# One TensorE product per Householder reflection, an eigenvalue search by leading minors in two rounds, and new intervals between the small products

## The reference

```
x = x + L0(h)   # normalized adjacency, W1, batch norm, relu, W2, batch norm
x = x + L1(h)   # two graph convolutions, then four LSTMs over windows of 1, 2, 3, 4 nodes
x = x + L2(h)   # U (relu((U^T h) W1 + b1) W2 + b2), U the eigenvectors of the 64x64 normalized Laplacian
x = x + L3(h)   # three convolutions with adj*adj: W1 (256), W2 (512), W3 (128)
```

## Time and profile before

| what | value |
|---|---|
| median of 3 runs | 1024.05 us (1023.99 to 1024.16) |
| profiled execution | 1024.09 us, span 1022.3 us, mean granted clock 0.950 |
| PE busy | 861.4 us (84%) |
| DVE busy | 591.2 us (58%) |
| ACT busy | 527.1 us (52%) |
| POOL busy | 333.1 us (33%) |

### The profile page before, as it was taken

One profiled execution on the slowest core, in us unless ns is written; L12 is line 12 of the kernel. 1 busy time (PEld: TensorE's weight loads), 2 busy tenths in 40 slices (PEclk: granted clock), 3 DMA queues, 4 the chain that ended last, 5 costly groups with the idle time before them and its releaser, 6 DMA issues.

```text
span 1022.3 us, 12192 instructions
## 1 busy us (share of the span) xinstructions
PE 861.4 (84%) x3721; PEld 569.7 (56%) x3721; DVE 591.2 (58%) x2897; ACT 527.1 (52%) x962; POOL 333.1 (33%) x404
## 2 busy tenths in 40 slices
PE   2678578298979999799877989966899999999998
...
DMA packets 2961, 13.26 MB, mean 13 GB/s; under 512 B 464, under 2 KB 464, under 8 KB 2640
## 3 DMA queue, kind: packets, MB, share of 16 engines
...
## 4 chain that ended last, share of the span: by engine, by line
PE 55%; DVE 27%; POOL 8%; ACT 7%; issue 3%; DMA 0%; SPq 0%; DVEq 0%; ACTq 0%; POOLq 0%
PE PS L390 54%; POOL BIG L853 7%; ACT T L756 2%; DVE ST L1361 2%; ACT BIG L795 1%; DVE stats L1333 1%; DVE Fq L1170 1%; DVE Fq L1167 1%; DVE PS L1119 1%; ACT BIG L787 1%; DVE sc L1050 1%; ACT BIG L772 1%; DVE vcol L1047 1%; DVE T L1457 1%; DVE PS L1123 1%
## 5 line engine op out<-in xcount | busy, mean ns | idle before, releaser
L390 PE MATMUL PS<-BIG,wts 128*128 128x512 f32 (+2 forms) x1264 | 438.1, 500 | 37.6 <-POOL BIG L853 21.8
L390 PEld LDWEIGHTS PS<-BIG,wts 128*128 128x128 f32 x1264 | 239.9, 195 | 198.1 <-issue 112.7
L853 POOL TENSOR_TENSOR BIG<-BIG 128x256 f32<-128x256 f32 (+2 forms) x272 | 254.8, 943 | 247.8 <-ACT BIG L787 183.0
L787 ACT ACTIVATE BIG<-PS,lbias 128x256 f32<-128x256 f32 (+2 forms) x312 | 165.2, 558 | 102.6 <-PE PS L390 102.0
L694 ACT ACTIVATE BIG<-PS 128x1024 f32<-128x1024 f32 x64 | 65.5, 1023 | 88.9 <-PE PS L390 88.9
L694 ACT ACTIVATE T<-PS 128x512 f32<-128x512 f32 x96 | 55.1, 593 | 98.6 <-PE PS L390 98.6
L702 ACT ACTIVATE T<-X,shift,rstd 128x128 f32<-128x128 f32 x192 | 78.3, 482 | 52.4 <-DVE shift L1349 52.4
L1472 DVE TENSOR_TENSOR X<-X,PS 128x512 f32<-128x512 f32 x64 | 43.4, 682 | 107.1 <-PE PS L390 87.1
L390 PE MATMUL PS<-T,wts 128*128 128x512 f32 x192 | 100.3, 653 | 1.0 <-ACT T L694 0.7
L1493 DVE TENSOR_TENSOR T<-PS,wts 128x512 f32<-128x512 f32 x16 | 11.1, 691 | 150.9 <-PE PS L390 150.9
L841 POOL TENSOR_SCALAR rstd<-mv 128x4 f32<-128x4 f32 x48 | 10.9, 228 | 234.6 <-DVE mv L1340 234.6
...
## 6 DMA issues: line engine op xcount, KB each, us to landing
X<-x_in SPq DMA_DIRECT2D x1, 4096.0 KB, 12.8
...
```

The source lines that it names most:

```text
L390: return nc.tensor.matmul(o, l, r, start=start, stop=stop)
L787: nc.scalar.activation(LB[:, q, {"i": I_, "g": G_, "f": F_, "o": O_}[g], 0:n], PS[:, 3 * q + rank[q] % 3, 0:n], ACT.Tanh if g == "g" else ...
L853: nc.gpsimd.tensor_tensor(out, a, b, op).then_inc(pool_set[q], 1)
```

## The change

One product per reflection: `row_product` and NI are gone. The next pivot row is computed on VectorE, from the old row of S (which TensorE brings together with the av product, `old_row`) and the two rank-one terms of the present reflection; the norm and the other sums are made from it on VectorE, and the updates of S run beside the next reflection (`update`, `aside`). The search has two rounds: the first spreads 4096 shifts over all partitions and counts for all eigenvalues at once, the second looks at 64 shifts for each. Leading minors (products, rescaled once half way) take the place of quotients, without a reciprocal in each step. The factorizations from both ends run as one chain, the lower 64 partitions forwards and the upper 64 backwards, in four segments with rescaling; one more product (`ways`) brings both to all partitions. The planner's intervals and its prices of the LSTM products are new. The order of layer 1's own work, layers 2 and 3 and all DMAs but the size of the constants are as before.

```diff
-ROUNDS = 3
+ROUNDS = 2
...
-PACE = 2.5
-PACE_ROW = 1.8
-PACE_AV = 4.9
-PACE_GRID = 38.0
-PACE_TWIST = 45.0
+PACE = 3.0
+PACE_AV = 8.0
+PACE_GRID = [40.0, 32.0]
+PACE_TWIST = 27.0
+PACE_SCAN = 13.0
+SMALL = 0.5
+SHORT_ROUND = 1.6
...
-            def row_product(k):
-                pe.wait_ge(hh_x, k + 1)
-                mm(eb(0)[:, 0:NODES + 1 - k], S[0:NODES, k:k + 1].broadcast_to((NODES, P)),
-                   NI[0:NODES, k + 1:NODES + 2]).then_inc(hh_row, 1)
+            def old_row(o, k):
+                n = NODES - 1 - k
+                return mm(o[:, 0:n], ident[0:NODES, k:k + 1].broadcast_to((NODES, P)), S[0:NODES, k + 1:NODES])
             def av_product(k):
                 pe.wait_ge(hh_v, k + 1)
+                if k + 1 < REFLECTIONS:
+                    old_row(eb(3), k + 1)
                 mm(eb(2)[:, 0:NODES - k], vcol[0:NODES, 0:1].broadcast_to((NODES, P)), S[0:NODES, k + 1:NODES + 1])\
                     .then_inc(hh_av, 1)
...
-                    yield PACE_ROW
-                    row_product(k)
                     yield PACE_AV
                     av_product(k)
...
-                    yield PACE_GRID
+                    yield PACE_GRID[n]
                     pe.wait_ge(grid_cnt, n + 1)
-                    mm(eb(2)[:, 0:1], C("fold"), sc[:, 3:4]).then_inc(grid_sum, 1)
+                    if n == 0:
+                        mm(eb(2)[:, 0:1], tmp[:, :], ones[:, 0:1]).then_inc(grid_sum, 1)
+                    else:
+                        mm(eb(2)[:, 0:1], C("fold"), sc[:, 3:4]).then_inc(grid_sum, 1)
...
                 yield PACE_TWIST
+                pe.wait_ge(prep_dve, PREP["ways"])
+                prep(mm(eb(0)[:, 0:P], C("fold"), both_ways[:, :]))
+                yield PACE_SCAN
...
+            old_row(eb(0), 0).then_inc(hh_row, 1)
...
-                row_product(r)
...
+                clock[0] += SMALL
                 due[0] = None if pace is None else max(due[0], clock[0] - 1.0) + pace
...
-                            spend(n * 4 * (1 + (s > 0)) / 2400)
+                            spend(n * 4 * (2 if s else 1.25) / 2400)
+                        if s == 0 and p > 2:
+                            spend(SHORT_ROUND)
...
+            def update(k, in_psum):
+                trail = S[:, k + 1:NODES]
+                z = (eb(1) if in_psum else zrow)[:, 0:NODES - 1 - k]
+                first = op(v.scalar_tensor_tensor(trail, z, vn, trail, ALU.mult, ALU.add))
+                yield
+                dve.wait_ge(hh_ops, first)
+                op(v.scalar_tensor_tensor(trail, row_of(k, in_psum), zn, trail, ALU.mult, ALU.add))
+                yield
...
-                head, trail = S[:, k:k + 1], S[:, k + 1:NODES]
-                v0, vr, av = eb(0)[:, 0:1], eb(0)[:, 0:m], eb(2)[:, 0:m]
-                xm = NI[:, NODES:NODES + 1]
-                dve.wait_ge(hh_S, k + 1)
-                v.tensor_scalar(NI[:, NODES:NODES + 2], C("below")[:, k:k + 2], head, None, ALU.mult)\
-                    .then_inc(hh_x, 1)
...
-                small_product()
-                dve.wait_ge(hh_row, k + 1)
-                copied = v.tensor_copy(sc[:, 36:38], eb(0)[:, m:m + 2])
...
+                xr, trail = row_of(k, False), S[:, k + 1:NODES]
+                x0 = xr[:, 0:1]
+                vr = xr if by_pool else row_of(k, True)
...
+                def aside():
+                    behind = update(k - 1, k > REFLECTED) if k else iter(())
+                    next(behind, None)
+                    rest = op(v.tensor_tensor_reduce(junks[:, 0, 0:m - 1], xr[:, 1:m], vr[:, 1:m], 1.0, 0.0, ALU.mult,
+                                                     ALU.add, r2))
+                    yield
+                    op(v.tensor_scalar(sg, x0, 0.0, 2.0, ALU.is_gt, ALU.mult))
+                    yield
+                    next(behind, None)
+                    yield
+                    op(v.tensor_tensor_reduce(junks[:, 1, 0:m], vr, ident[:, k + 1:NODES], 1.0, 0.0, ALU.mult, ALU.add, xc))
+                    yield
+                    dve.wait_ge(hh_ops, rest)
+                    op(v.tensor_scalar(guard, r2, TINY, 1e30, ALU.is_lt, ALU.mult))
+                    yield
+                off = aside()
+                squares = v.tensor_tensor_reduce(junks[:, 2, 0:m], xr, vr, 1.0, 0.0, ALU.mult, ALU.add, n2)
                 if by_pool:
-                    copied.then_inc(hh_norm2, 1)
+                    squares.then_inc(hh_norm2, 1)
+                    for _ in off:
+                        next(beside, None)
+                    next(beside, None)
+                    next(beside, None)
+                    dve.wait_ge(hh_norm, k + 1)
+                    need(hh[0], beside)
                 else:
-                    op(copied)
...
+                    got = op(squares)
+                    next(off)
+                    need(got)
+                    got = op(v.tensor_scalar(y_.bitcast(I32), n2.bitcast(I32), -0.5, float(0x5F3759DF), ALU.mult, ALU.add))
+                    next(off)
+                    need(got)
...
-                op(v.tensor_scalar(vcol[:, :], C("next")[:, k:k + 1], beta, xm, ALU.mult, ALU.subtract))
-                op(v.tensor_scalar(v0, v0, beta, None, ALU.add))
-                sync()
...
-                v.tensor_tensor_reduce(junk[:, 0:m], trail, vr, 1.0, 0.0, ALU.mult, ALU.add, S[:, NODES:NODES + 1])\
...
+                v.tensor_tensor_reduce(junks[:, 3, 0:m], trail, vr, 1.0, 0.0, ALU.mult, ALU.add, S[:, NODES:NODES + 1])\
...
-                sync()
...
-                op(v.tensor_scalar(vcn, vcol[:, :], nc_, -1.0, ALU.mult, ALU.mult))
-                dve.wait_ge(hh_v, k + 1)
...
-                op(v.tensor_scalar(wp, S[:, NODES:NODES + 1], nc_, -1.0, ALU.mult, ALU.mult))
-                sync(1)
-                op(v.tensor_scalar(vcnn, vcn, nc_, -1.0, ALU.mult, ALU.mult))
...
+                need(op(v.tensor_scalar(hd, x0, beta, guard, ALU.mult, ALU.max)), beside)
+                need(op(v.reciprocal(nc_, hd)), beside)
+                op(v.tensor_scalar(half_nc, nc_, -0.5, None, ALU.mult))
+                op(v.tensor_scalar(a0, x0, nc_, -1.0, ALU.mult, ALU.mult))
+                op(v.tensor_scalar(vn, vcol[:, :], nc_, -1.0, ALU.mult, ALU.mult))
...
-                op(v.tensor_scalar(wcol[:, :], vcnn, eb(2)[:, m:m + 1], wp, ALU.mult, ALU.add))
-                op(v.scalar_tensor_tensor(trail, av, vcn, trail, ALU.mult, ALU.add))
-                sync()
-                v.scalar_tensor_tensor(trail, vr, wcol[:, :], trail, ALU.mult, ALU.add).then_inc(hh_S, 1)
+                dve.wait_ge(hh_v, k + 1)
+                need(hh[0])
+                need(op(v.tensor_scalar(kappa, eb(2)[:, m:m + 1], half_nc, None, ALU.mult)), beside)
+                got = op(v.scalar_tensor_tensor(zrow[:, 0:m], xr, kappa, eb(2)[:, 0:m], ALU.mult, ALU.add))
+                op(v.tensor_scalar(zc, vcol[:, :], kappa, S[:, NODES:NODES + 1], ALU.mult, ALU.add))
+                need(got, beside)
+                psum = k + 1 > REFLECTED
+                if k + 1 < REFLECTIONS:
+                    op(v.tensor_scalar(b0, zrow[:, 0:1], nc_, -1.0, ALU.mult, ALU.mult))
+                    got = op(v.scalar_tensor_tensor(eb(1)[:, NODES:NODES + m - 1], zrow[:, 1:m], a0, eb(3)[:, 0:m - 1],
+                                                    ALU.mult, ALU.add))
+                    if psum:
+                        op(v.scalar_tensor_tensor(eb(1)[:, 0:m], xr, kappa, eb(2)[:, 0:m], ALU.mult, ALU.add))
+                    need(got, beside)
+                    for p_ in range(2 if k + 1 >= REFLECTED else 1):
+                        got = op(v.scalar_tensor_tensor(row_of(k + 1, p_), xr[:, 1:m], b0, eb(1)[:, NODES:NODES + m - 1],
+                                                        ALU.mult, ALU.add))
+                    op(v.tensor_scalar(zn, zc, nc_, -1.0, ALU.mult, ALU.mult))
+                    need(got, beside)
+                else:
...
+                    gop(v.memset(Z[:, HALF, :], 1.0))
+                    gop(v.tensor_scalar(xn, C("grid" if r else "spread"), s1(2), s1(1), ALU.mult, ALU.add))
                     gsync()
-                    gop(v.tensor_tensor(Qh[:, :, :], eb(0)[:, 0:NODES].unsqueeze(2).broadcast_to([P, NODES, M]),
-                                        xg[:, :].unsqueeze(1).broadcast_to([P, NODES, M]), ALU.subtract))
+                    gop(v.tensor_scalar(Z[:, HALF - 1, :], xn, d[:, 0:1], None, ALU.add))
+                    gop(v.tensor_scalar(Z[:, HALF + 1, :], xn, d[:, NODES - 1:NODES], None, ALU.add))
+                    for i in range(1, HALF):
+                        j = NODES - 1 - i
+                        up, dn = HALF - i, HALF + i
+                        gsync(1)
+                        gop(v.scalar_tensor_tensor(ta, xn, d[:, i:i + 1], Z[:, up, :], ALU.add, ALU.mult))
+                        gsync(1)
+                        gop(v.scalar_tensor_tensor(tb, xn, d[:, j:j + 1], Z[:, dn, :], ALU.add, ALU.mult))
```

(89 more changed lines are left out.)

200 lines of the change are left out of this document (102 added, 98 removed).

## The result

| | before | changed |
|---|---|---|
| median, us | 1024.06 (1023.99 to 1024.16, 4 runs) | 1056.45 (1055.23 to 1064.93, 4 runs) |
| ratio | | 1.0334, 95% interval 1.0280 to 1.0388 |
| profiled execution, us (its span) | 1024.1 (1022.3) | 1064.9 (1063.1) |
| TensorE busy, us | 861.4 | 878.7 |
| VectorE busy, us (instructions) | 591.2 (2897) | 616.1 (3415) |

The changed kernel is 32.4 us slower, against a forecast of 35.4. A group of layer 1 is counted from its first product to that of the next.

What follows compares the result with a forecast made beforehand. VectorE was taken to bound layer 0's first pass, a ring of dependencies its second, and TensorE's order layer 1, with its end exposed. 22 + 1 + 2 + 5 + 14 - 8.6 = +35.4 gave 1059.5 us, range 1029 to 1080.

Steps and rivals of the forecast that it cites:

- First pass, +22: Layer 0 up to 119.5 us: VectorE's additional instructions cost 1.05 us in each of 21 reflections, +22 us (2 to 38).
- Second pass, +1: Layer 0, 132 to 180 us: a turn stays at 5.6 to 5.7 us, +1 us over nine turns (-3 to +5).
- The ring: Layer 0's second pass: vcol product, w2, ScalarE copy, statistics, rest of the reflection, next vcol product; 5.62 us a turn.
- Layer-1 reflections, +2: Layer 1: TensorE's stalls for reflections grow from 3.9 to about 6 us, +2 us (-3 to +8).
- Search, +5: Layer 1's eigenvalue search: TensorE stalls 12.8 us against 7.6 at the first count, +5 us (0 to +10); second round nothing.
- Minors and V, +14: Layer 1's last group: stalls of 16.3 us for leading minors and 1.3 for V, less 3.5 now, +14 us (+7 to +21).
- Tail, -8.6: End of layer 1: the next statistics start behind the last addition, at 686.0 and not 694.62 us, -8.6 us.
- B: Rival: layer 1 hides its chains, leading-minor steps cost the lower bound and additions fill pauses; 1035 us, chance 0.17.
- C: Rival: layer 0's new instructions fit in its pauses and a reflection doesn't grow; 1011 us, chance 0.12.
- D: Rival: VectorE's two-source SBUF reads block in layer 0, +0.7 us in each of 21 reflections; 1074 us, chance 0.07.
- E: Rival: TensorE's load is unchanged and losses and gains cancel; 1024 us, chance 0.03.

Runs made afterwards that it cites:

- e7: The kernel before with four more independent one-column VectorE instructions in each of layer 0's 31 reflections: 1034.11 us, ratio 1.0103.
- e1: The changed kernel run again with no edit: 1058.95 us, ratio 1.0342; its profiled execution took 1063.06 us.
- e5: The changed kernel with product intervals 53, 46, 46, 17 and 6, and layer 1's VectorE instructions placed by measured durations: 1030.00 us, ratio 1.0062.

## Why the forecast was right, and where it wasn't

**First pass, +22.** The mechanism is shown: ordinary turns are 6.25 to 6.3 us where 6.3 was forecast, and e7 gives 0.12 us for each independent one-column instruction, as the sum had it (0.10 to 0.13). In the execution of e1, with three single slow turns, the pass is 19.3 us longer; with eight, seven of them in rows, 27.5. The term left the clock out: I took the granted clock of the earlier trace rows as given. When the clock has dropped the turn is TensorE's (0.66 + 0.64 + 2.07 + 0.69 + 3.78, less overlaps, 7.49 us) and no longer VectorE's.

**Second pass, +1.** It came out at -1.8: turns of 5.38 in place of 5.62. The ring keeps its links, and the trace takes it apart: from the end of the last statistics to the next product are 1.40 us where 1.85 were (the forecast had 1.35 for 1.7), and from the first product of a turn to the ScalarE copy 2.58 where 2.36 were, so old_row costs 0.22 and not the 0.35 that I had let eat the gain. Within the bounds.

**Layer-1 reflections, +2.** Stalls for the reflections were to grow from 3.9 to 6 us; they are 4.0. Groups 1 and 2 together are 1.5 us shorter here, but 2.1 us longer in the other execution of the same kernel (252.2). The eight traces with the new reflection in layer 1 have 246.9 to 252.2 us for the two groups, the three with the old one at its old places 249.2 to 250.1. So neither the loss that I forecast nor a gain is shown.

**Search, +5.** The stall seems sized to 0.2 us (13.0 against 12.8), and part of that is luck: the 12.8 stood against 4.6 + 3.0, whose counterpart is 13.0 + 1.0, and both of its sides were too short. From the diagonals' product to that of the count are 54.5 us (502.39 to 556.89; forecast 50.5), and TensorE's own work in them is 40.5 (forecast 37.7). The third group grew by 10.2: 8.6 from these waits and the late state addition at its end (13.0 + 1.0 + 2.2 against 4.6 + 3.0), 1.7 from waits for GpSimd and ScalarE and 1.3 from longer matmuls, which I had at nothing, less 1.4 of waits for reflections. That the second count has no stall was right too.

**Minors and V, +14.** The fourth group grew by 15.4. A minor's step is 0.43 us (forecast 0.40), V waits 1.9 (1.3). Instead of a 16.3 us pause there are 10.5 us in three pieces: from the second count's product (597.0) to `ways` (640.1) VectorE takes 42.8 us (forecast 45.5), and TensorE's work, slow matmuls included, covers 32.6 (forecast 29.2). What the sum lacked is TensorE's own time, 8.1 us more in the group, and a wait of 3.9 us at the last product: 13 short steps of VectorE stand in an interval of 3. Waits for GpSimd are 2.2 us shorter. So this term has its mechanism, and its size comes from other parts than forecast.

**Tail, -8.6.** As forecast: the statistics start behind the last addition, and the gap of 8.6 us is gone.

**The rivals.** B (layer 1 hides its chains, 1035) fails as a statement on the changed kernel and is almost exactly what e5 reaches by moving products: the chains of layer 1 can be hidden, but not by the intervals of the change. C (new instructions fit in pauses) falls with e7. D (two-input reads in layer 0): the sums over `xrow` take 0.19 to 0.23 us in layer 0, 0.14 to 0.19 with one input in PSUM in layer 1, no 0.7, also beside an instruction of GpSimd (0.19 at 177.99 us, GpSimd 177.98 to 178.58). The same mechanism is real in the third group of layer 1, where I hadn't looked for it, at 3 to 4 us. E is out. So the forecast of 1059.5 holds with its largest terms in their places. That it comes within about 3 us of the median is partly luck: in the profiled execution the terms are off by up to 5.5 us each, with either sign, and their sum is 5.2 us too low, while the median is 8.5 us below that execution and was not profiled.
